# Rounding feed-forward rows in one VectorE pass to 16-bit integers

## The reference

```python
x = x + xattn(layernorm(x), ctx, ...)     # fake-quantised cross attention, 16 heads of 32
x = x + attn(layernorm(x), ...)           # latent attention with low-rank projections, 16 heads of 128
x = x + ffn(layernorm(x), w_gate, w_up, w_down)
```

```python
def act_quant(x):                  # per row, 8 bits
    scale = 128.0 / clip(max(abs(x), axis=-1), 1e-5)
    return clip(round(x * scale), -128, 127) / scale
def weight_quant(w):               # ternary
    scale = 1.0 / clip(mean(abs(w)), 1e-5)
    return clip(round(w * scale), -1, 1) / scale
def bitlinear(x, w):   return act_quant(x) @ weight_quant(w).T
def h_bitlinear(x, w): return act_quant(fwht(x)) @ weight_quant(w).T   # Walsh-Hadamard transform first
gate, up = bitlinear(x, w_gate), bitlinear(x, w_up)      # 512 -> 2048
return h_bitlinear(silu(gate) * up, w_down)              # 2048 -> 512
```

## Time and profile before

| | us |
|---|---|
| median of 3 executions | 582.42 |
| lowest and highest of them | 581.97 and 582.75 |
| profiled execution: its span, from the first to the last instruction | 582.8 |

### The profile page before, as it was taken

One profiled execution on the slowest core, in us unless ns is written; L12 is line 12 of the kernel. 1 busy time (PEld: TensorE's weight loads), 2 busy tenths in 40 slices (PEclk: granted clock), 3 DMA queues, 4 the chain that ended last, 5 costly groups with the idle time before them and its releaser, 6 DMA issues. The chain is left out here.

```text
span 582.8 us, 10649 instructions
## 1 busy us (share of the span) xinstructions
PE 531.9 (91%) x4283; PEld 333.8 (57%) x4286; DVE 457.6 (79%) x858; ACT 364.7 (63%) x431; POOL 28.4 (5%) x28
## 2 busy tenths in 40 slices
PE   3999999999899999999998788699999899996995
PEld 2444555543566656665665565488884565652582
DVE  2599999966899989998999797401593889878995
ACT  5624656464799889988998788400343753586342
POOL 0300000000300200030005100000000000000000
PEclk9999999999999999999998788899999999997999
DMA  8723300042345435553556459603938204300000
GB/s 319 264 74 87 130 1 1 0 142 85 119 148 182 165 107 176 166 168 112 160 177 241 170 165 432 265 1 95 319 163 341 106 0 180 111 0 0 2 2 36
DMA packets 20145, 78.84 MB, mean 135 GB/s; under 512 B 2176, under 2 KB 3200, under 8 KB 16896
## 3 DMA queue, kind: packets, MB, share of 16 engines
q1 hardware_dynamic: 20096, 78.16, 37.8%
HBM read 75.27 MB, written 0.79 MB: 131 GB/s over the span
## 5 line engine op out<-in xcount | busy, mean ns | idle before, releaser
L1122 DVE CUSTOM_DVE_ANT_0 arena<-ps,arena 128x1024 f32<-128x1024 f32 x128 | 152.5, 1220 | 16.2 <-issue 7.7
L1530 ACT ACTIVATE arena<-arena,small 128x4096 int16<-128x4096 f32 x32 | 121.5, 3798 | 2.5 <-DVE small L1135 2.4
L600 PE MATMUL ps<-arena 128*128 128x512 f16 x384 | 100.1, 380 | 0.0
L641 PE MATMUL ps<-small,arena 128*128 128x128 bf16 x1024 | 81.7, 225 | 8.1 <-DVE arena L1142 4.8
L566 PE MATMUL ps<-arena 128*128 128x512 f16 x384 | 85.2, 379 | 1.2 <-DVE arena L1053 1.2
L641 PEld LDWEIGHTS ps<-small,arena 128*128 128x128 bf16 x1024 | 61.1, 100 | 17.8 <-issue 6.9
L1537 ACT ACTIVATE arena<-ps 128x512 int32<-128x512 int32 x96 | 56.9, 593 | 21.7 <-PE ps L641 21.3
L815 PE MATMUL ps<-arena 128*128 128x256 f32 (+1 forms) x288 | 67.3, 397 | 0.7 <-ACT arena L1619 0.7
L815 PEld LDWEIGHTS ps<-arena 128*128 128x128 f32 x288 | 55.7, 194 | 11.8 <-issue 3.3
L566 PEld LDWEIGHTS ps<-arena 128*128 128x128 f16 x384 | 37.2, 98 | 43.6 <-issue 1.5
L657 PEld LDWEIGHTS ps<-arena 128*128 128x128 f16 x1024 | 43.0, 97 | 30.1 <-issue 8.2
(11 more groups left out here) (172 smaller groups left out, 729.5 us busy)
## 6 DMA issues: line engine op xcount, KB each, us to landing
arena<-key_scales SPq DMA_DIRECT2D x64, 512.0 KB, 5.0
arena<-in_ctxT SPq DMA_DIRECT2D x8, 1024.0 KB, 6.8
arena<-in_wg SPq DMA_DIRECT2D x4, 1024.0 KB, 7.2
arena<-in_wo SPq DMA_DIRECT2D x2, 2048.0 KB, 11.6
arena<-in_wu SPq DMA_DIRECT2D x4, 1024.0 KB, 6.9
arena<-in_wd SPq DMA_DIRECT2D x4, 1024.0 KB, 5.8
arena<-in_wuq SPq DMA_DIRECT2D x1, 3072.0 KB, 24.9
arena<-in_wkr SPq DMA_DIRECT2D x1, 2048.0 KB, 13.9
```

Source lines behind the costliest of these rows:

```text
L600: last = pe.matmul(ps[:, bank, :], wv16[wpart][:, k, g * P:(g + 1) * P], ctx16[cpart][:, k, tok], start=(k == 0 and i == 0), stop=(k == KC ...
L641: last = pe.transpose(ps[:, bank, :].bitcast(BF16)[:, b * P:(b + 1) * P], p16[u % 2][:, (8 * q + b) * P:(8 * q + b + 1) * P].bitcast(BF16) ...
L1122: dve.tensor_tensor_reduce(sc[:, u % 2, i * SCW:(i + 1) * SCW], ps[:, 2 * (n % 2):2 * (n % 2) + 2, :].rearrange("p a b -> p (a b)"), skb[: ...
L1530: act.activation(p16[u % 2], sc[:, u % 2, :], ACT.Exp, bias=ebias[:, u % 2:u % 2 + 1], scale=sq[:, i:i + 1], accum_out=rsum[:, u:u + 1]).t ...
```

## The change

The two-pass rounding becomes one pass. `to_units` now multiplies by the scale, takes the minimum with 127 and writes 16-bit integers; the conversion of the result to an integer is what rounds. `clip` is gone. ACT's multiply-add for the second half of tile 1 is gone, with the two semaphores `asc` and `yun` that served it, DVE's increment of `asc`, its wait for `yun`, and ACT's wait for `asc`. PE turns the 16-bit integers with their bits read as bfloat16, and the copies out of PSUM (three by ACT, one by DVE, and the two `store_xiT`) read them as 16-bit integers and write bfloat16. The number of transposes, copies and matmuls and their sizes stay.

```diff
-        xi = at(rest + 11776, [QT, D], BF16)
+        xi = at(rest + 11776, [QT, D], I16)
...
-        ti = at(o_tail + 16384, [QT, I], BF16)
+        ti = at(o_tail + 16384, [QT, I], I16)
...
-        asc, yun = sem("row_scales"), sem("y_in_units_by_act")
...
-                                        xi[:, t, k * P:(k + 1) * P], idb[:, :])
+                                        xi[:, t, k * P:(k + 1) * P].bitcast(BF16), idb[:, :])
...
-            def to_units(src, t):
-                return dve.tensor_scalar(src, src, ascale[:, t:t + 1], MAGIC, ALU.mult, ALU.add)
-
-            def clip(dst, src):
-
-                return dve.tensor_scalar(dst, src, MAGIC + 127.0, -MAGIC, ALU.min, ALU.add)
+            def to_units(dst, src, t):
+
+                return dve.tensor_scalar(dst, src, ascale[:, t:t + 1], 127.0, ALU.mult, ALU.min)
...
-                link(to_units(xn3[:, t, :], t))
-                clip(xi[:, t, :], xn3[:, t, :]).then_inc(xis, 1)
+                to_units(xi[:, t, :], xn3[:, t, :], t).then_inc(xis, 1)
...
                 scales_of(slice(t, t + 1))
-                dve.sem_inc(asc, 1)
                 for half in range(2):
                     part = slice(half * I // 2, (half + 1) * I // 2)
-                    if half and t:
-                        dve.wait_ge(yun, 1)
-                    else:
-                        link(dve.tensor_scalar(y_sb[:, t, part], y_sb[:, t, part], ascale[:, t:t + 1], MAGIC,
-                                               ALU.mult, ALU.add))
-                    clip(ti[:, t, part], y_sb[:, t, part]).then_inc(tis, 1)
+                    to_units(ti[:, t, part], y_sb[:, t, part], t).then_inc(tis, 1)
...
-                            ps[:, 1, :].bitcast(BF16).rearrange("p (a b) -> p a b", a=8)).then_inc(tid, 1)
+                            ps[:, 1, :].bitcast(I16).rearrange("p (a b) -> p a b", a=8)).then_inc(tid, 1)
...
-                if t:
-                    act.wait_ge(asc, t + 1)
-                    act.activation(y_sb[:, t, I // 2:], y_sb[:, t, I // 2:], ACT.Identity, scale=ascale[:, t:t + 1],
-                                   bias=magic[:, 0:1]).then_inc(yun, 1)
...
-                                   ps[:, half, :].bitcast(BF16).rearrange("p (a b) -> p a b", a=8),
+                                   ps[:, half, :].bitcast(I16).rearrange("p (a b) -> p a b", a=8),
```

More of the change, by code:

```diff
@@ L944, in turn_ti @@
                         last = pe.transpose(ps[:, half, :].bitcast(BF16)[:, b * P:(b + 1) * P],
-                                            ti[:, t, (8 * half + b) * P:(8 * half + b + 1) * P], idb[:, :])
+                                            ti[:, t, (8 * half + b) * P:(8 * half + b + 1) * P].bitcast(BF16),
+                                            idb[:, :])
                     last.then_inc(tit, 1)
@@ L1672, in store_xiT @@
                 act.activation(xiT[:, :, t * P:(t + 1) * P],
-                               ps[:, 4 + 3 * t, :].bitcast(BF16)[:, 0:D].rearrange("p (k a) -> p k a", k=KC),
+                               ps[:, 4 + 3 * t, :].bitcast(I16)[:, 0:D].rearrange("p (k a) -> p k a", k=KC),
                                ACT.Copy).then_inc(xie, 1)
```

## The result

The changed kernel took 580.51 us, the median of 9 executions (578.40 to 581.33); the kernel before, beside it, 582.42 (581.97 to 583.61, also 9). The ratio of the times is 0.995, with a 95% interval of 0.9929 to 0.9971: faster by 0.3 to 0.7%. The medians lie 1.9 us apart, the means 2.65 (582.63 and 579.98). The forecast was 579.8, and a gain of 2.65. The median lies inside the range for 8 in 10, 579.1 to 581.0, but just above the forecast's own range, 579.2 to 580.4, and within 0.1 us of the 580.6 of the rival with a late tail; so the time alone does not tell these two apart.

The account below looks back on a forecast made before the run. VectorE's rounding was taken to set the pace, for tile 0 at the first rounding and both tiles at the second. Gains of 0.35 + 2.3 = 2.65 us off the 582.42 median gave 579.8; 8-in-10 range 579.1 to 581.0.

Parts of the forecast that it names:

- the forecast's own range: Whole kernel: 579.2 to 580.4 us, for the case of doubled rate and a free tail, given 80%.
- the rival with a late tail: Second rounding: y's last copy late or TensorE needing time between its parts; gain about 1.8 us, 580.6; chance 6%.
- The new instruction: VectorE's tensor-scalar from float32 to int16, at both roundings: 0.75 us for 1024 columns, 0.48 for 512.
- the forecast's x: Pace of the new instruction at 1024 columns in the second rounding: 0.67 us, with the second rounding's gain 5.01 - 4x.
- The second rounding: VectorE's rounding before the last matmuls: 1.56 us saved from tile 0 and 0.77 from tile 1, taken as 2.3.
- The three conditions: Second rounding: TensorE free in time, y's last copy not late (0.67 us in hand), copies out of PSUM no slower.
- The first rounding: Tile 0's rounding before the gate matmuls: 0.47 us earlier on VectorE, of which 0.35 reaches silu.
- its lower end: First rounding: full clock returns at its old instant near 534.1, so the 0.47 us gained are worth 0.23.
- Tile 1's saving: First rounding: 0.47 us on VectorE worth nothing, lengthening its 0.31 us wait for silu; in full if VectorE came last.
- the pace of 1.2 us: Both roundings: int16 output loses the doubled rate, x 1.145; gain 0.6 us, 581.8, no measurable change; chance 9%.
- the 2.1 of a slower conversion: Both roundings: new instruction at half the int16 row's rate, x 2.1; kernel slower, 586.0 us; chance 3%.
- The rival with a clock that stays low longer: First stage: eight more matmuls at half speed cost 1.8 us; gain near 1.0, 581.4, no change; chance 2%.

Follow-up runs that it names:

- the repeat of the changed kernel: The changed kernel run and profiled once more, nothing altered; median 580.08 us, ratio 0.995 to the kernel before.
- the second-only kernel: Against the kernel before, only the second rounding in one pass, ScalarE's multiply-add gone; median 580.13 us, ratio 0.996.
- the kernel made to have 1.2: The changed kernel with its one pass made of an instruction with two tensor inputs; median 582.47 us, ratio 0.9991 to the kernel before.
- the first-only kernel: Against the kernel before, only the first rounding in one pass, the second with ScalarE's multiply-add as before; median 582.50 us, ratio 0.9995.

## Why the prediction was right

**The new instruction** was forecast at 0.75 and 0.48 us, and takes 0.749 and 0.485; the pair's 1.42 gives a pace of 0.67, the forecast's x. Writing int16 does not slow a tensor-scalar. The Trainium skill ("VectorE: DVE Perf Modes", section "Mode 2×_2P") gives an instruction with one tensor input between SBUF and SBUF two elements a cycle, in float32 too, and names no condition on the output's type; the trace agrees for int16, and with a second tensor input the same work took 1.281 us.

**The second rounding** was forecast at 1.56 + 0.77 and gave 1.57 + 0.78 in the changed kernel's trace. Alone it gave 2.31; there the first rounding took 0.03 more than in before. The three conditions that it named held: TensorE was free in time (its 2.19 us are gone, and the loads of its transposes wait for VectorE and not the reverse), y's last copy was not waited for, and the copies kept their length. That ScalarE's multiply-add was free to remove is shown by the kernel that keeps it: 0.23 us, and not its 1.24.

**The first rounding** was the term that was mis-sized: 0.35 forecast, 0.43 measured. Of the two ways that the term allowed, the clock took that of its lower end, a return that does not follow the work. Full speed came back at 534.16 us of the trace before and at 534.01 of the trace after, although the row of gate matmuls had moved from 531.15 to 529.47. Behind tile 0's reciprocal that is 6.04 and 7.11 us, and in the repeat of the changed kernel it is 6.43. The instants are worked out from the half microsecond in which the granted clock lies between its two levels: 0.84 from 534.0 in before, and in the changed kernel, its repeat and the second-only kernel

```profile
534.00:534.50 0.50, 0.50 (x3) 0.99 0.00 0
...
532.00:532.50 0.50, 0.50 (x3) 0.67 0.00 0
...
531.50:532.00 0.50, 0.50 (x3) 0.52 0.00 0
```

The Trainium skill ("TensorE: Matmul & The Clock Gate", Part 1) has the gate's schedule run freely, and these instants fit.

But this way did not cost half of the 0.47. What releases silu is the eighth matmul; the line of the changed kernel names VectorE's increment for tile 1, but the kernel that gives tile 1 its two passes back has silu as soon, 5.86 us behind the reciprocal. The price holds only if the moved matmuls ran at full speed before, and none of those ahead of silu did. The rows at 531.15 and 529.47 hold 15 of 16 matmuls: the trace has no record of the first, so they begin with the second. Where all sixteen are recorded, silu comes 3.67 us behind the first, in the repeat of the changed kernel (531.76 - 528.09) as in the second-only kernel (531.81 - 528.14). From the second matmul it is 534.42 - 531.15 = 3.27 us before and 532.77 - 529.47 = 3.30 after. The loads of their weights are 0.427 us apart, so the eighth matmul of before ended near 531.15 + 7 x 0.427 = 534.14, just as the clock rose: all eight ran at half speed in both kernels, and only 0.03 us was lost. Against the second-only kernel, which has the two passes and whose clock returned later (531.98, 6.50 behind the reciprocal), the one pass saves the full 0.47: silu comes there 531.81 - 525.48 = 6.33 us behind the reciprocal, and 5.86 in the repeat. So the middle value, 0.35, came near in part by luck: its lower end was priced wrong, and either end gives nearly 0.47. I had priced the 0.47 us by the clock alone, and not by the work that stood between its start and the release.

**Tile 1's saving** at the first rounding is worth nothing with the wait before the first product there, and 0.36 us with that wait gone. The prediction had it count in full, 0.47, in that case.

**The base of the sum.** I set the profiled execution's span, 582.8, beside the median of 582.42 and called it 0.4 above. The results after show that a time is its execution's span plus 1.8 (580.55 for a span of 578.8). The profiled execution of before was thus one of some 584.5 us by my estimate, two above the median. It did no harm, since what it had lost lay ahead of the reciprocal, and the sum was taken off the median; but the difference of the two profiled spans, 4.0 us, overstates the change by 1.2, the two reciprocals' difference. The spread was set too small: the forecast's own range took 0.4 us either side from three executions, and the changed kernel's nine spread over 2.9.

The rivals: the pace of 1.2 us did not occur, nor the 2.1 of a slower conversion, and the kernel made to have 1.2 shows what it would have given, 0.37 us. No copy or transpose was late in the tail. The rival with a clock that stays low longer came in part: measured from the reciprocal the return was 1.07 us later than before, so more matmuls behind the first eight ran at half speed. It cost nothing, because the second silu waits for ScalarE's own pass of 2.08 us behind the first: the two silus lie 2.57 us apart in both traces (534.42 and 536.99; 532.77 and 535.34).

## What to carry to other kernels

When a two-pass rounding becomes one pass, ask first at which pace the one instruction runs: with one tensor input it kept its pace into int16 (749 ns for 1024 columns) and was worth 2.8 us; with two inputs (1281 ns) the same saving of instructions was worth 0.4. Follow a saved time to the instruction that releases the next engine, and price it by the work in between. Compare traces over the part that a change can touch: here it was 51.85 and 51.86 us in two executions of the changed kernel, while whole times spread by 3.

## What was not expected of the hardware

Filling the idle time of TensorE at the first rounding with useless matmuls is worth 1.3 us in the changed kernel, and nothing in the kernel before, where the clock then fell behind a later gap; with that gap filled too it is worth 54.63 - 53.72 = 0.91. The later gap was 2.19 us long in the kernel before and in the first-only kernel without a fall (the last 24 matmuls took 5.34 us in both), and 2.20 with one (7.03): in these traces the length of a gap alone does not tell whether the clock falls. The change removes that gap, and so also what it might cost.
